# Recurrent linear-attention block: the orders of all engines written anew, and one wait of GpSimd drawn from its own order

## The reference, cut to what matters

```python
xn = layernorm(x)
q, k, v = split(xn @ Wqkv + bqkv)
qp, kp = elu(q) + 1, elu(k) + 1
kv = kp.T @ v                       # one 256 x 256 matrix for each of 8 batches
attn = (qp @ kv) / (qp @ sum(kp) + 1e-6)
z = layernorm(xn + attn) * g1 + b1
ffn = (silu(z @ Wg + bg) * (z @ Wu + bu)) @ Wd + bd     # hidden width 682
s = layernorm(z + ffn) * g2 + b2
gate = silu(xn @ ternary(weight).T)
out = x + s * gate
```

## Time and profile before

| what | value |
|---|---|
| median of three runs | 1268.01 us |
| the profiled execution's own time | 1268.96 us |
| its span from first to last instruction | 1267.2 us |
| TensorE busy | 1237.6 us, 98% |
| VectorE, ScalarE, GpSimd busy | 1023.5, 948.4, 805.9 us |
| mean granted TensorE clock | 0.994 |

### The profile page before, as it was taken

How to read it: one execution, slowest core, us unless ns; L and a number is a source line. 1 busy time by engine, 2 the same in 40 slices (tenths; PEclk the granted TensorE clock), 3 DMA queues, 4 the chain that set the end, 5 groups by cost and what they waited for, 6 DMA issues and landing times.

```text
span 1267.2 us, 24275 instructions
## 1 busy us (share of the span) xinstructions
PE 1237.6 (98%) x7747; PEld 1108.6 (87%) x7747; DVE 1023.5 (81%) x2442; ACT 948.4 (75%) x1540; POOL 805.9 (64%) x994
## 2 busy tenths in 40 slices
...
DMA packets 96435, 84.16 MB, mean 66 GB/s; under 512 B 9907, under 2 KB 88629, under 8 KB 96310
## 3 DMA queue, kind: packets, MB, share of 16 engines
...
...
## 4 chain that ended last, share of the span: by engine, by line
PE 91%; POOL 3%; DVE 3%; issue 2%; ACT 1%; DMA 0%; POOLq 0%; DVEq 0%; ACTq 0%
PE bank L1137 62%; PE d_bank L1137 18%; PE xk_bank L1137 7%; PE bank L1151 3%; POOL rz L581 0%; DVE st L838 0%; POOL rz L587 0%; POOL rz L574 0%; POOL rz L568 0%; DMA xa<-in_L_attn_x_dram 0%; POOL rz L605 0%; POOL rstd L535 0%; DVE kp L906 0%; DVE qp_l L934 0%; DVE wgu_l L1092 0%
## 5 line engine op out<-in xcount | busy, mean ns | idle before, releaser
L1137 PE MATMUL bank<-zT_h,wgu_h 128*128 128x512 f32 x704 | 279.1, 396 | 0.1
L1137 PE MATMUL bank<-zT_l,wgu_h 128*128 128x512 f32 x704 | 278.7, 396 | 0.0
L1137 PE MATMUL bank<-zT_h,wgu_l 128*128 128x512 f32 x704 | 278.3, 395 | 0.0
L568 POOL TENSOR_TENSOR rz<-rz,g2b 128x256 f32<-128x256 f32 x124 | 110.3, 890 | 138.9 <-ACT rz L639 138.5
L1137 PE MATMUL d_bank<-wd_h,h_h 128*128 128x256 f32 x640 | 182.8, 286 | 0.0
L558 POOL TENSOR_TENSOR ksum<-ksum,kp 128x256 f32<-128x256 f32 x120 | 97.0, 809 | 134.0 <-DVE kp L913 132.8
L1137 PE MATMUL d_bank<-wd_l,h_h 128*128 128x256 f32 x640 | 180.6, 282 | 0.0
L1137 PE MATMUL d_bank<-wd_h,h_l 128*128 128x256 f32 x640 | 180.3, 282 | 0.0
L639 ACT ACTIVATE hs<-bank,hb 128x512 f32<-128x512 f32 x192 | 130.9, 684 | 64.1 <-PE bank L1137 63.0
L1137 PEld LDWEIGHTS bank<-zT_l,wgu_h 128*128 128x128 f32 x704 | 132.3, 188 | 31.7
L1137 PEld LDWEIGHTS bank<-zT_h,wgu_h 128*128 128x128 f32 x704 | 132.3, 188 | 25.5 <-DVE kv_l L1040 1.7
...
## 6 DMA issues: line engine op xcount, KB each, us to landing
...
```

Of the source, the lines that this page charges most:

```text
L568: eng.tensor_tensor(row_, row_, g2b[:, :], ALU.mult).then_inc(S["a"], 1)
L1137: ins = eng.matmul(dst, left, right, start=first and n == 0, stop=last and n == len(pairs) - 1, **kw)
```

## The change

No instruction of arithmetic is added or taken away, and TENSOR_JOBS and END_JOBS stay as they are. New are the eleven other orders, one wait and one way to count a wait. The diff, with the first parts of the FILL orders cut:

```diff
 SCALAR_STEPS = steps("""
-    zT_high 0, xk_copy 0, zT_high 1, q_exp 0, q_exp 1, kv_high 0, q_high 0, k_exp 0, q_high 1,
-    kv_high 1, silu_gate 0, k_high 0, silu_gate 1, h_high 0, x_res 0, h_high 1, x_res 1, silu_tern 0,
-    last_rows 0, silu_gate 2, x_res 2, k_exp 1, last_rows 1, h_high 2, x_res 3, silu_tern 1,
-    silu_gate 3, last_rows 2, k_high 1, h_high 3, silu_gate 4, x_high 0, z_rows 0, x_high 1,
-    last_rows 3, silu_gate 5, z_rows 1, z_rows 2, z_rows 3, h_high 4, xn_high 0, h_high 5, xn_high 1""")
+    xk_copy 0, zT_high 0, zT_high 1, q_exp 0, kv_high 0, q_exp 1, q_high 0, kv_high 1, k_exp 0,
+    silu_gate 0, q_high 1, silu_gate 1, h_high 0, h_high 1, silu_gate 2, last_rows 0, x_res 0, x_res 1,
+    x_res 2, last_rows 1, silu_tern 0, k_exp 1, h_high 2, last_rows 2, x_res 3, last_rows 3, k_high 0,
+    silu_gate 3, silu_tern 1, k_high 1, silu_gate 4, z_rows 0, xn_high 0, x_high 0, h_high 3, z_rows 1,
+    silu_gate 5, h_high 4, z_rows 2, z_rows 3, x_high 1, xn_high 1, h_high 5""")
 VECTOR_STEPS = steps("""
-    zT_low 0, zT_low 1, k_add 0, a_stats 0, q_elu 0, kv_bias 0, ffn_rows 0, kv_bias 1, kv_low 0,
-    q_elu 1, k_add 1, q_low 0, ffn_rows 1, k_max 0, q_low 1, kv_low 1, last_stats 0, h_rows 0, h_rows 1,
-    h_low 0, last_shift 0, h_low 1, attn 0, attn 1, h_rows 2, a_norm 0, x_turn 0, attn 2, h_low 2,
-    attn 3, k_low 0, q_aggregate 0, h_rows 3, k_max 1, k_low 1, attn_norm 0, x_low 0, h_low 3, x_low 1,
-    h_rows 4, h_rows 5, h_low 4, h_low 5""")
+    zT_low 0, a_stats 0, zT_low 1, q_elu 0, kv_bias 0, kv_low 0, k_add 0, kv_bias 1, ffn_rows 0,
+    q_elu 1, ffn_rows 1, kv_low 1, q_low 0, k_add 1, last_stats 0, h_rows 0, h_rows 1, q_low 1, h_low 0,
+    last_shift 0, k_max 0, h_low 1, attn 0, h_rows 2, attn 1, a_norm 0, x_turn 0, h_low 2, attn 2,
+    k_low 0, k_max 1, attn 3, q_aggregate 0, k_low 1, h_rows 3, attn_norm 0, h_rows 4, h_low 3,
+    h_rows 5, x_low 0, h_low 4, x_low 1, h_low 5""")
 GPSIMD_STEPS = steps("""
-    xn_low 0, sum_k 0, last_rstd 0, a_rstd 0, xn_low 1, z_g1 0, last_gain 0, last_gain 1, z_g1 1,
-    z_g1 2, sum_k 1, z_g1 3, last_offset 0, last_offset 1, last_gate 0, q_rstd 0, last_gate 1,
-    last_gain 2, last_add 0, last_gain 3, last_offset 2, last_gate 2, last_add 1, last_offset 3,
-    last_add 2, sum_k 2, tail_again 0, last_gate 3, sum_k 3, tail_again 1, last_add 3""")
+    a_rstd 0, xn_low 0, z_g1 0, last_rstd 0, last_gain 0, last_offset 0, xn_low 1, last_gain 1,
+    last_gate 0, last_gain 2, last_offset 1, last_gate 1, last_offset 2, last_add 0, last_gain 3,
+    q_rstd 0, last_gate 2, sum_k 0, last_add 1, last_offset 3, sum_k 1, last_gate 3, sum_k 2, z_g1 1,
+    tail_again 0, z_g1 2, tail_again 1, last_add 2, last_add 3, sum_k 3, z_g1 3""")
 END_SCALAR = steps("""
-    zT_high 0, zT_high 1, silu_gate 0, last_rows 0, h_high 0, silu_gate 1, last_rows 1, h_high 1,
-    silu_gate 2, h_high 2, last_rows 2, silu_gate 3, last_rows 3, silu_gate 4, h_high 3, h_high 4,
+    zT_high 0, zT_high 1, silu_gate 0, silu_gate 1, h_high 0, last_rows 0, last_rows 1, last_rows 2,
+    h_high 1, silu_gate 2, last_rows 3, h_high 2, silu_gate 3, silu_gate 4, h_high 3, h_high 4,
     silu_gate 5, h_high 5""")
 END_VECTOR = steps("""
-    zT_low 0, zT_low 1, ffn_rows 0, ffn_rows 1, last_stats 0, last_shift 0, h_rows 0, h_low 0, h_rows 1,
+    zT_low 0, zT_low 1, ffn_rows 0, ffn_rows 1, last_stats 0, h_rows 0, h_low 0, last_shift 0, h_rows 1,
     h_low 1, h_rows 2, h_low 2, h_rows 3, h_low 3, h_rows 4, h_low 4, h_rows 5, h_low 5""")
 END_GPSIMD = steps("""
-    z_g1 0, last_rstd 0, z_g1 1, end_terms 0, last_gain 0, last_offset 0, z_g1 2, last_gate 0,
-    last_gain 1, last_gain 2, last_offset 1, last_gain 3, last_gate 1, z_g1 3, last_add 0, tail_again 0,
-    tail_again 1, last_offset 2, last_add 1, last_gate 2, last_offset 3, last_add 2, last_gate 3,
+    z_g1 0, z_g1 1, z_g1 2, z_g1 3, last_rstd 0, end_terms 0, last_gain 0, last_gain 1, last_offset 0,
+    last_offset 1, last_gain 2, last_gate 0, last_offset 2, last_add 0, last_gate 1, last_gate 2,
+    last_gain 3, tail_again 0, tail_again 1, last_offset 3, last_add 1, last_add 2, last_gate 3,
     last_add 3""")
 FILL_JOBS = fill("""
-    TX 0 0, warm 9 1, TX 0 1, K 0 0, K 0 1, XK 0 0, TX 1 0, warm 9 2, TX 1 1, XK 0 1, XK 0 2, XK 0 3,
-    K 1 0, K 1 1, warm 9 0, setup_bias_0 0 0, TX 2 0, setup_bias_1 0 0, XK 1 0, TX 2 1, XK 1 1, K 2 0,
-    XK 1 2, XK 1 3, K 2 1, TX 3 0, setup_bias_2 0 0, XK 2 0, TX 3 1, setup_sum 0 0, K 3 0, XK 2 1,
-    XK 2 2, K 3 1, XK 2 3, XK 3 0, XK 3 1, setup_transposes 0 0, TX 4 0, TX 4 1, Q 0 0, XK 3 2, XK 3 3,
-    Q 0 1, KV 0 0, KV 0 1, K 4 0, B 0 0, K 4 1, B 0 1, N 0 0, N 0 1, N 0 2, N 0 3, XK 4 0, XK 4 1,
-    XK 4 2, XK 4 3, TZ 0 0, TZ 0 1""")
+    TX 0 0, TX 0 1, K 0 0, K 0 1, TX 1 0, warm 9 1, TX 1 1, warm 9 2, XK 0 0, XK 0 1, K 1 0, XK 0 2,
+    XK 0 3, K 1 1, TX 2 0, setup_bias_0 0 0, K 2 0, TX 2 1, XK 1 0, XK 1 1, XK 1 2, XK 1 3, K 2 1,
+    TX 3 0, setup_bias_1 0 0, TX 3 1, XK 2 0, XK 2 1, K 3 0, XK 2 2, XK 2 3, K 3 1, TX 4 0,
+    setup_sum 0 0, setup_bias_2 0 0, XK 3 0, TX 4 1, XK 3 1, Q 0 0, XK 3 2, Q 0 1, XK 3 3,
+    setup_transposes 0 0, K 4 0, K 4 1, KV 0 0, KV 0 1, B 0 0, N 0 0, N 0 1, N 0 2, N 0 3, XK 4 0,
+    XK 4 1, B 0 1, warm 9 0, XK 4 2, XK 4 3, TZ 0 0, TZ 0 1""")
 FILL_SCALAR = fill("""
...
-    xn_high 4 1, xT_high 4 1, q_exp 0 0, xk_copy 0 0, q_high 0 0, q_exp 0 1, x_res 0 0, x_res 0 1,
-    kv_high 0 0, kv_high 0 1, x_res 0 2, q_high 0 1, k_exp 4 0, k_exp 4 1, silu_tern 0 0, x_res 0 3,
-    k_high 4 0, silu_tern 0 1, k_high 4 1, z_rows 0 0, z_rows 0 1, z_rows 0 2, z_rows 0 3, x_high 5 0,
-    x_high 5 1, xn_high 5 0, xn_high 5 1""")
...
+    xT_high 4 0, k_exp 3 1, xn_high 4 0, setup_row_2 0 0, q_exp 0 0, xn_high 4 1, xT_high 4 1,
+    q_exp 0 1, xk_copy 0 0, setup_gu_high_1 0 0, q_high 0 0, q_high 0 1, k_exp 4 0, x_res 0 0,
+    x_res 0 1, kv_high 0 0, k_high 4 0, kv_high 0 1, x_res 0 2, k_exp 4 1, x_res 0 3, setup_d_high 0 0,
+    k_high 4 1, silu_tern 0 0, silu_tern 0 1, z_rows 0 0, z_rows 0 1, z_rows 0 2, z_rows 0 3,
+    x_high 5 0, x_high 5 1, xn_high 5 0, xn_high 5 1""")
 FILL_VECTOR = fill("""
-    a_stats 0 0, setup_k_low 0 0, a_norm 0 0, setup_bk 0 0, xT_low 0 0, a_stats 1 0, xT_low 0 1,
-    k_add 0 0, k_add 0 1, k_max 0 0, a_norm 1 0, k_max 0 1, xT_low 1 0, a_stats 2 0, xT_low 1 1,
...
-    q_elu 0 0, setup_ternary_parts 0 0, kv_bias 0 0, setup_gu_low_1 0 0, kv_bias 0 1, q_elu 0 1,
-    kv_low 0 0, k_add 4 0, kv_low 0 1, q_low 0 0, q_low 0 1, k_max 4 0, k_add 4 1, attn 0 0,
-    setup_hidden_biases 0 0, a_norm 5 0, x_turn 5 0, attn 0 1, attn 0 2, attn 0 3, k_low 4 0,
-    q_aggregate 0 0, k_max 4 1, attn_norm 0 0, k_low 4 1, setup_d_tail 0 0, x_low 5 0, x_low 5 1""")
+    a_stats 0 0, a_norm 0 0, setup_k_low 0 0, xT_low 0 0, a_stats 1 0, xT_low 0 1, setup_bk 0 0,
+    k_add 0 0, a_norm 1 0, k_add 0 1, setup_bq 0 0, k_max 0 0, xT_low 1 0, k_max 0 1, a_stats 2 0,
...
+    xT_low 4 0, setup_ternary 0 0, k_max 3 1, setup_gu_low_0 0 0, a_stats 5 0, q_elu 0 0, xT_low 4 1,
+    q_elu 0 1, setup_ternary_parts 0 0, k_add 4 0, a_norm 5 0, q_low 0 0, q_low 0 1, kv_bias 0 0,
+    k_max 4 0, kv_bias 0 1, k_add 4 1, kv_low 0 0, k_low 4 0, kv_low 0 1, x_turn 5 0, k_max 4 1,
+    attn 0 0, attn 0 1, attn 0 2, attn 0 3, q_aggregate 0 0, attn_norm 0 0, k_low 4 1,
+    setup_gu_low_1 0 0, x_low 5 0, x_low 5 1, setup_d_tail 0 0, setup_hidden_biases 0 0""")
 FILL_GPSIMD = fill("""
...
-    sum_k 1 1, sum_k 1 2, sum_k 1 3, a_rstd 3 0, sum_k 2 0, sum_k 2 1, sum_k 2 2, setup_d_low 0 0,
-    a_rstd 4 0, sum_k 2 3, sum_k 3 0, sum_k 3 1, sum_k 3 2, sum_k 3 3, a_rstd 5 0, xn_low 4 0,
-    sum_k 4 0, xn_low 4 1, sum_k 4 1, q_rstd 0 0, sum_k 4 2, sum_k 4 3""")
...
+    sum_k 3 0, sum_k 3 1, sum_k 3 2, xn_low 4 0, a_rstd 5 0, xn_low 4 1, sum_k 3 3, sum_k 4 0,
+    sum_k 4 1, setup_d_low 0 0, sum_k 4 2, sum_k 4 3, q_rstd 0 0""")
 def tail_again(g, n):
...
-                eng.wait_ge(S["ks"], min(TILES * (g + LEAD) + before_tail("sum_k", g, n), TILES * GROUPS))
-                if g:
-                    eng.wait_ge(S["c"], TILES * (g - 1) + before_tail("last_gate", g, n))
+                before, count = before_tail(g, n)
+                if count:
+                    eng.wait_ge(S[before], count)
 def k_add(g, p):
...
                 eng.wait_ge(S["K"], n + 1)
+                if n == 0:
+                    eng.wait_ge(S["w_bk"], 1)
```

More of the change, by code:

```diff
@@ L130 @@
-    XK 4 2, XK 4 3, TZ 0 0, TZ 0 1""")
-FILL_SCALAR = fill("""
-    setup_k_high 0 0, xT_high 0 0, setup_q_high 0 0, xT_high 0 1, k_exp 0 0, k_exp 0 1, xT_high 1 0,
-    setup_abs 0 0, xT_high 1 1, k_exp 1 0, k_exp 1 1, xT_high 2 0, setup_gu_high_0 0 0, setup_row_0 0 0,
-    xT_high 2 1, setup_gu_high_1 0 0, k_exp 2 0, setup_d_high 0 0, k_exp 2 1, setup_row_1 0 0,
-    xT_high 3 0, xT_high 3 1, setup_row_2 0 0, k_exp 3 0, k_exp 3 1, xn_high 4 0, xT_high 4 0,
-    xn_high 4 1, xT_high 4 1, q_exp 0 0, xk_copy 0 0, q_high 0 0, q_exp 0 1, x_res 0 0, x_res 0 1,
```

(3 more changed lines are left out.)

31 lines of the change are left out of this document (22 added, 9 removed).

## The result

The kernel after takes 1254.42 us (median of 4 runs, 1253.81 to 1254.66), the kernel before 1268.24 us beside it: a ratio of 0.9892, 95% interval 0.9875 to 0.9909. That is 13.8 us less, where 4.8 were forecast, and it lies outside the range. Direction and place of the first gain were right; a second, as large, was said not to exist.

What follows compares the result with a forecast made beforehand. TensorE, busy 1237.6 of 1267.2 us, was taken as the bound, leaving only opening and end to win. Opening 5.7, less 0.8 hand-overs, less 0.3 steady, plus 0.2 end: 4.8 us, so 1263.2 us, range 1260.2 to 1267.3.

Steps and rivals of the forecast that it cites:

- Part 5: Steady iterations: the new orders win at most 0.2 us and can only lose more; 0.3 us of loss taken.
- The bounds taken: Steady iterations: loss between 0 (each step fits) and 9.3 us (N 0 late by 0.3 us in 31 iterations).
- The sign set for this part: Steady iterations: TensorE's waits from 85 to 1230 us stay under 1 us in all.
- Part 6: The end: reordered last steps of GpSimd and VectorE gain 0.2 us, bounds -0.5 and 0.7.
- Part 1: Opening up to XK 3 3: it ends at 50.9 us, 55.0 before for like work; gain 4.1 us.
- Part 2: From XK 3 3 to the first numerator: N 0 0 at 59.7 us behind a 2.4 us wait; gain so far 2.5.
- Part 3: From the numerators to the steady order: N's wait for sg goes; steady products begin at 74.3 for 79.99, 5.7 us earlier.
- The 0.8 us for hand-overs: Opening: 0.8 us taken off the gain for semaphore latencies and GpSimd and VectorE in each other's way.
- Part 4: The clock: half clock stays for XK 4 2 to TZ, 4.6 us; at full clock it becomes 2.3.
- rival A: Opening, XK 4 2 to TZ: the clock stays at 1.00, 2.3 us more gain, 1260.9 us; chance 0.15.
- Rival B: Opening stays VectorE's: products up to XK 3 3 wait as now, 4.1 us not gained, 1267.3 us; chance 0.15.
- Rival C: Steady iterations: N 0 late by 0.3 us in each of 31, 9.3 us slower, 1272.5 us; chance 0.10.

Runs made afterwards that it cites:

- z1: Kernel before with one swap in ScalarE's steady order: z_rows 1 ahead of silu_gate 5; 1264.24 us, ratio 0.9970.
- kvlow_z1: z1 with kv_low 1 moved directly behind q_elu 1 in VectorE's steady order; 1272.19 us, ratio 1.0028 against the kernel before.
- warm_first: Kernel after with the warm product warm 9 1 back between TX 0 0 and TX 0 1, as in the kernel before; 1253.39 us.
- b1_first: Kernel after with B 0 1 directly behind B 0 0, ahead of the numerators, as in the kernel before; 1257.15 us, ratio 0.9913.
- d_early: Kernel after with setup_d_high behind setup_row_2 on ScalarE and setup_d_low behind sum_k 3 3 on GpSimd; 1255.19 us, ratio 0.9899.
- warm_back: Kernel after with the warm product warm 9 0 back behind K 1 1 instead of between B 0 1 and XK 4 2; 1254.33 us.

## Why the prediction was wrong

**Part 5 is the step that failed**: "the new steady orders can win at most 0.2 us and can only lose more". It was read from the earlier trace rows, a view that lists only idle time. A product that starts late while its forerunner is in flight leaves none. By TensorE's products the steady iterations and iteration 31 gave 6.6 us, in three parts:

- 0.13 us at each TZ 0, for z_rows 1: 31 x 0.13 = 4.0. z1 shows it in each of its ordinary iterations; its median, 3.9 less, agrees within 2.3 to 5.5.
- 0.18 us more in each of six batch iterations and 0.4 in iteration 27: 1.5. In the six, 0.1 is at U 1, which kvlow_z1 shows. The rest is at N 0, and is read from the times.
- 1.1 us at D 5 and G 0 of iteration 31. They lie behind the end of the window of the earlier trace rows, and the steady orders alone take them away.

The bounds taken, 0 and 9.3 us of loss, both had the wrong side. The sign set for this part, waits of TensorE under 1 us, came true (there are none) and couldn't have shown the failure, as it is the same view. The new order was followed against iteration 8 place by place (h_low 0 was given 0.14 us before N 0 and had 0.19), the old one wasn't: it would have shown z_rows 1 ending 0.14 us before TZ 0. And iteration 8 ends no batch.

**Part 6 was mis-sized**: 0.2 us forecast, 0.9 measured behind the last product. That GpSimd's steps end sooner was right; that they hold VectorE's last rows while they run (2.13 for 1.67) wasn't in it.

**Part 1** forecast XK 3 3 to end at 50.9; it ended at 52.5, still free of waits. The difference is K 0 0, K 0 1 and TX 1 0 at the long pitch: I took the end of K 0 1 at 15.11 "in both", though the new order takes the warm product from in front of them. With it back (warm_first) XK 3 3 ends at 50.94, as forecast. **Part 2** had N 0 0 at 59.7 behind a wait of 2.4; it was 61.1 and 2.16, the same 1.4 us late.

**Part 3** has 5.7 us; the first steady product came 6.8 us sooner (72.82 for 79.64; the 79.99 of the earlier trace rows is where the transposes end). That this is near is partly luck: the numerator was 1.4 us late, the chain from it to the end of k_low 4 1 took 8.9 us where 9.9 were summed, and from there to the steady products it was 2.8 instead of 4.6. N's wait for sg is gone, as said, and that B 0 1 stands behind the numerators is why (b1_first). It missed that silu_tern 0 0 waits for setup_d_low, since both use one buffer; the 1.21 us of B 0 1 are from that. They cost 0.4 at most (d_early, where that wait is gone, has 11.3 for 11.7 us), as the attention chain on VectorE is almost as long. The 0.8 us for hand-overs had no row to pay them.

**Part 4** kept half clock for XK 4 2 to TZ, and **rival A** came true: 1.00 from 68 us on. From XK 4 2 to the first steady product it is 2.70 us (70.12 to 72.82) where it was 4.29 at 0.50 (75.35 to 79.64), so 1.6 of A's 2.3 us were there. What kept the clock up is open: warm_back shows only that the moved warm product didn't. **Rival B** is refuted by the opening. **Rival C** didn't occur: in the kernel after h_low 0 ends 0.19 to 0.20 us before N 0 in all iterations. That a later h_low 0 would cost its full delay, kvlow_z1 shows.
